# Window attention on one core: scores and query-key in 64x64 tiles, relative bias added by VectorE, maximum subtracted by GpSimd

## The chip, the cores and the metric

The kernel runs on 1 core of one Trainium2 chip. The time is device microseconds of one execution; the measure is the median over several executions of the same program. Everything is in 32-bit floats. In the text PE is TensorE, DVE is VectorE, ACT is ScalarE, POOL is GpSimd and SP is SyncE, which here only issues DMAs.

## What is computed

One transformer block with 8x8 windows on an image batch `x` of 4x48x128x128, and behind it an inverted-bottleneck convolution. The change touches only the attention of the first block (window size `ws` 8, 4 heads of 12 channels, 64 tokens a window):

```
h = _layernorm(xf, norm1_g, norm1_b)            # then cut into windows: (windows, 64, 48)
qkv = h @ qkv_w.T + qkv_b
q, k, v = (qkv[0] * scale, qkv[1], qkv[2])
attn = jnp.einsum('whnd,whmd->whnm', q, k)
attn = attn + rpb_table[rel_idx].transpose(2, 0, 1)[None]
attn = jax.nn.softmax(attn, axis=-1)
o = jnp.einsum('whnm,whmd->whnd', attn, v)
o = o.transpose(0, 2, 1, 3).reshape(B_, N, C) @ proj_w.T + proj_b
xf = shortcut + o                               # windows put back
m = _layernorm(xf, norm2_g, norm2_b)
xf = xf + gelu(m @ fc1_w.T + fc1_b) @ fc2_w.T + fc2_b
...
x + bn(conv1x1(relu(bn(dwconv3x3(relu(bn(conv1x1(x))))))))
```

## The kernel before

The program has three stages one after another: `attention`, `mlp`, and the convolution. `attention` works on 128 groups of 8 windows (512 tokens). A group is 4 pairs of windows; a pair fills the 128 partitions with its 2x64 tokens. Each engine has its own list of instructions, a function `step(i)` that is run for i = -4 to 130, with semaphores between the engines. In one step an engine works on several groups at different points of the pipeline: the layer norm of group i+4 and i+3, query and key of group i+2, the softmax of group i, the weighing of values of group i-1, the output of group i-2, and the second layer norm of group i-3. The order inside a step is written out by hand. The first ten steps (-4 to 5) and the last nine are written out; those between run in a loop of two steps (`schedule`, L200).

The steps that the change touches:

- *Query and key.* PE multiplies the normalized, transposed tokens `xnT` with `w_qk` (L369), two row tiles of 64 rows and 112 columns. The result is copied from PSUM twice: q by DVE into `qa` (L438), k by ACT into `kk` (L491).
- *Keys.* For the scores of all four heads in one matmul, the keys are laid out block by block: SP copies, with one DMA per head (L295), the 12 rows of a head from `kk` to the head's columns in `kb`, 12 partitions x 8 windows x 64 tokens.
- *Bias.* `kb` holds 128 rows: 64 of the bias, which are written once, and 48 of keys. `qa` holds an identity above q. So the matmul of the scores (L329), 128 rows by 64 columns, 256 moving columns, adds the bias itself. Eight such matmuls make the scores of a group in PSUM (`ps_s`, two banks), four at the end of the step before and four at the start of the group's own step.
- *Softmax.* DVE takes the maximum of each row of 64 from PSUM (L421) and subtracts it while it moves the scores into `prob` (L428). ACT takes the exponential in one instruction (L496). PE turns the probabilities (L317), ACT copies them out (L456), PE weighs the values (L381).
- *Others in a step.* ACT also copies the values (L465), the turned output `oT` (L469), the turned tokens `xnT` (L472), and makes the two steps of the layer norms (logarithm L475, root L484). PE turns the output (L339) and the tokens (L346), projects the output (L359), and makes the values (L388). POOL does four small products of the layer norms (L506, L511, L515, L520). SP stores the finished group (L290) and loads a coming one (L178).

A matmul in 32 bits is two instructions in the profile, a transpose is one.

Of the kernel before, what the change touches and what calls it, by code (L numbers as in the profile page):

```python
# [9 lines left out]
ALU = mybir.AluOpType  # L10
# [3 lines left out]
P = 128  # L14
# [5 lines left out]
ONE = 64  # L20
# [95 lines left out]
def attention(nc, d):  # L116

    with ExitStack() as ctx:
        sb = lambda n, s, t=F32: ctx.enter_context(nc.sbuf_tensor(n, s, t))
        sem = lambda n: ctx.enter_context(nc.semaphore(n))  # L120
        ident = sb("ident", [P, P])
        eps = sb("eps", [P, 1])
        w_qk, w_v, w_o = sb("w_qk", [P, 112]), sb("w_v", [P, 2 * C]), sb("w_o", [P, 2 * C])
        qkv_w, qkv_b = sb("qkv_w", [P, 3 * C]), sb("qkv_b", [1, 3 * C])
        lnrow, qk_row = sb("lnrow", [1, 3 * C]), sb("qk_row", [1, 112])
# [5 lines left out]
        cen, cen2 = ([sb(f"{n}{s}", [P, PAIRS, C]) for s in range(2)] for n in ("cen", "cenb"))  # L131
        sq = sb("sq", [P, 2 * PAIRS, C])
        xn = [sb(f"xn{s}", [P, PAIRS, ONE]) for s in range(2)]
        xnT = [sb(f"xnT{s}", [P, TOK // 2]) for s in range(2)]


        qa = [sb(f"qa{s}", [P, TOK]) for s in range(2)]
        kk = [sb(f"kk{s}", [P, TOK]) for s in range(2)]
        kb = [sb(f"kb{s}", [P, 2 * PAIRS, NH, NT]) for s in range(2)]
        vb = [sb(f"vb{s}", [P, PAIRS, 2, 2, 2 * VE]) for s in range(2)]  # L140
        top = [sb(f"top{s}", [P, PAIRS * NH]) for s in range(2)]
# [11 lines left out]
        ps_a, ps_b = psum[:, 6, :], psum[:, 7, :]  # L153
        ps_xT, ps_v, ps_y = ps_a[:, 0:TOK // 2], ps_a[:, 0:PAIRS * C], ps_a[:, TOK // 2:TOK // 2 + PAIRS * C]
        ps_o, ps_oT = ps_b[:, 0:PAIRS * NH * VE], ps_b[:, TOK // 2:TOK]

        w_loaded, fixed, w_bias, w_ready = sem("w_loaded"), sem("fixed"), sem("w_bias"), sem("w_ready")
        ident_put, lnrow_put, row_put, rows_loaded = sem("ident_put"), sem("lnrow_put"), sem("row_put"), sem("rows_loaded")
# [7 lines left out]
        xnT_ready, xnT_copied, qk_ready, q_copied, k_copied = (  # L166
            sem(n) for n in ("xnT_ready", "xnT_copied", "qk_ready", "q_copied", "k_copied"))
        v_ready, v_copied, s_ready, top_done, sub_done, exp_done = (
            sem(n) for n in ("v_ready", "v_copied", "s_ready", "top_done", "sub_done", "exp_done"))
# [6 lines left out]
        def load_x(eng, g, s):  # L176

            eng.dma_start(xtok[:, bass.ds(g, 1), :, :], d["x_tokens"][:, bass.ds(g, 1), :, :]).then_inc(x_loaded[s], 16)  # L178

        def x_loads(g, s):  # L180

            return 8 * (g - s) + 16

        def x_of(g):
            return xtok[:, bass.ds(g, 1), :, :].rearrange("q g p c -> q (g p) c")

        def keys_of(i, s):

            return 16 * NH // 2 * (i - s) + 16 * NH

        def halves(t):

            return t.rearrange("q (a e t) -> q e a t", e=2, t=P)

        W_FIXED, FIXED = 3, 23

        def has(g):
            return not isinstance(g, int) or 0 <= g < GROUPS

        def schedule(eng, step, begin=None, at=0):  # L200

            for i in range(-4, 6):
                if begin and i == at:
                    begin(eng)
                step(i, i % 2)
            with eng.Fori(6, GROUPS - 7, 2) as i:
                step(i, 0)
                step(i + 1, 1)
            for i in range(GROUPS - 6, GROUPS + 3):
                step(i, i % 2)  # L210
# [3 lines left out]
        def shift_rows(pe):  # L214

            pe.wait_ge(w_loaded, 16 * W_LOADS)
            nc.tensor.matmul(ps_a[0:1, 0:3 * C], ln_b[:, :], qkv_w[0:C, :], start=True, stop=True).then_inc(w_bias, 1)
# [4 lines left out]
        def put_bias(eng, write, half):  # L222

            eng.wait_ge(looked_up, 1)
            eng.wait_ge(fixed, FIXED)
            cols = slice(NT // 2 * half, NT // 2 * half + NT // 2)
            found = psum[NT * half:NT * half + NT, half, 0:NH * NT // 2].rearrange("q (h m) -> q h m", h=NH)
            for s in range(2):
                write(kb[s][0:NT, :, :, cols], bc(found, 1, 2 * PAIRS)).then_inc(bias_put, 1)
# [1105 lines left out]
```

## Time and profile before

| | |
|---|---|
| median of 3 executions | 1934.54 us (1932.46 to 1935.5) |
| the profiled execution, its own time | 1930.68 us |
| its span, first to last instruction | 1928.8 us |
| PE busy over the span | 1834.6 us (95%) |
| DVE busy | 1447.5 us (75%) |
| ACT busy | 1307.4 us (68%) |
| POOL busy | 646.9 us (34%) |
| DMA queue q1 (SP and ACT issues) | 282114 packets, 189.12 MB |

The attention takes about the first 770 us of the span, the MLP stage the stretch to about 1050, and the convolution the rest. The shares of busy time over the span are averages over these three stages; what the change does is read from the first one alone. An engine's busy time counts instructions; the time that SP spends on issuing DMAs isn't counted as busy and is read from the rows of the DMA issues.

### The profile page before, as it was taken

How to read it: one execution, taken by the hardware profiler on the slowest of the kernel's cores; microseconds unless marked ns; L12 is line 12 of the kernel's file. 1: busy time of each engine (PE TensorE's matmuls, PEld its weight loads, DVE VectorE, ACT ScalarE, POOL GpSimd, SP SyncE). 2: the span in 40 equal slices, each digit the busy share in tenths (PEclk: the TensorE clock that was granted, in tenths of full speed). 3: DMA queues.
4: the chain of work that ended last, by engine and by line, in shares of the span. 5: the costliest groups of instructions: out<-in, count | busy, mean ns of one | idle time of the engine just before them, and what ended most of it. 6: DMA issues, size and time to landing. Idle time of an engine off the chain costs nothing.

```text
span 1928.8 us, 75776 instructions
## 1 busy us (share of the span) xinstructions
PE 1834.6 (95%) x30980; PEld 1570.3 (81%) x30980; DVE 1447.5 (75%) x2649; ACT 1307.4 (68%) x2838; POOL 646.9 (34%) x869
## 2 busy tenths in 40 slices
PE   5999999999999998789998999999999999999998
PEld 4888888888888886456666899999999999999997
DVE  5999999999999998667777566566566566566564
ACT  2888888888888786445555666666666666666665
POOL 4333333333333332502201443334243352343240
PEclk9999999999999999799999999999999999999999
DMA  2222222222222221778875354445364454545331
GB/s 68 69 74 76 74 77 74 77 77 74 78 73 78 73 78 64 163 182 186 184 176 130 83 136 103 98 132 107 96 146 94 115 121 105 111 128 102 101 109 35
DMA packets 286378, 198.91 MB, mean 103 GB/s; under 512 B 225928, under 2 KB 275610, under 8 KB 276442
## 3 DMA queue, kind: packets, MB, share of 16 engines
q1 hardware_dynamic: 282114, 189.12, 38.8%
q0 software_dynamic: 2368, 6.25, 1.7%
q8 instruction: 174, 2.85, 0.6%
q10 hardware_dynamic: 1688, 0.42, 0.1%
q14 instruction: 34, 0.28, 0.0%
HBM read 128.39 MB, written 54.72 MB: 95 GB/s over the span
## 4 chain that ended last, share of the span: by engine, by line
PE 51%; DMA 4%; ACT 2%; DVE 1%; issue 1%; SPq 0%; ACTq 0%; DVEq 0%
PE psum L1112 14%; PE psum L1131 14%; PE psum L1157 10%; PE psum L1166 5%; PE psum L632 3%; DMA room<-tok_mid 3%; PE psum L647 2%; PE psum L659 2%; ACT h2T L1213 1%; ACT h L870 1%; DVE room L697 0%; DVE room L708 0%; SPq L607 0%; ACTq L720 0%; DVE room L871 0%
## 5 line engine op out<-in xcount | busy, mean ns | idle before, releaser
L920 POOL TENSOR_TENSOR mats<-mats,dscale 112x2048 f32<-112x2048 f32 x72 | 260.8, 3622 | 315.9 <-DMA mats<-in_taps 313.3
L1112 PE MATMUL psum<-ew,xp 64*100 64x96 f32 x6144 | 322.2, 252 | 15.9 <-ACT h L870 13.6
L871 DVE TENSOR_SCALAR h<-psum 100x384 f32<-100x384 f32 x384 | 212.0, 557 | 150.2 <-PE psum L1112 138.3
L1112 PEld LDWEIGHTS psum<-ew,xp 64*100 64x100 f32 x6144 | 295.4, 165 | 25.2 <-ACT h L870 18.7
L1213 ACT ACTIVATE h2T<-psum 96x1024 f32<-96x1024 f32 x192 | 195.6, 1019 | 176.2 <-PE psum L1166 176.2
L1131 PE MATMUL psum<-h,mats 101*64 101x128 f32 x4608 | 269.3, 274 | 1.6 <-issue 0.9
L1131 PEld LDWEIGHTS psum<-h,mats 101*64 101x64 f32 x4608 | 252.0, 137 | 11.9 <-issue 2.0
L870 ACT ACTIVATE room<-psum 64x512 f32<-64x512 f32 (+1 forms) x384 | 206.1, 537 | 78.0 <-PE psum L1131 71.6
L329 PE MATMUL psum<-kb,qa 128*64 128x256 f32 x2048 | 244.0, 380 | 0.8 <-DVE prob L428 0.8
L871 DVE TENSOR_SCALAR room<-psum 64x512 f32<-64x512 f32 (+1 forms) x288 | 174.3, 605 | 64.7 <-PE psum L1131 58.8
L870 ACT ACTIVATE h<-psum 100x384 f32<-100x384 f32 x384 | 186.6, 486 | 48.4 <-PE psum L1112 34.2
L1157 PE MATMUL psum<-h2T,pw 128*64 128x128 f32 x3072 | 194.4, 276 | 9.1 <-ACT h2T L1213 9.0
L329 PEld LDWEIGHTS psum<-kb,qa 128*64 128x64 f32 x2048 | 140.7, 138 | 56.3 <-issue 1.9
L1157 PEld LDWEIGHTS psum<-h2T,pw 128*64 128x64 f32 x3072 | 167.2, 137 | 20.3 <-ACT h2T L1213 13.4
L511 POOL TENSOR_TENSOR xn<-cen,rstd 128x192 f32<-128x192 f32 x128 | 64.9, 507 | 338.8 <-ACT rstd L484 338.8
L421 DVE TENSOR_REDUCE top<-psum 128x16 f32<-128x1024 f32 x128 | 156.8, 1225 | 6.9 <-PE psum L329 4.7
L428 DVE TENSOR_TENSOR prob<-psum,top 128x1024 f32<-128x1024 f32 x128 | 155.9, 1218 | 0.1
L894 POOL COPY xp<-piece 128x400 f32<-128x400 f32 x128 | 67.5, 528 | 256.5 <-DMA piece<-img_mid 241.1
L456 ACT ACTIVATE probT<-psum 128x512 f32<-128x512 f32 x256 | 151.2, 601 | 0.0
L381 PEld LDWEIGHTS psum<-vb,probT 128*64 128x64 f32 x4096 | 129.9, 138 | 18.6 <-issue 1.2
L381 PE MATMUL psum<-vb,probT 128*64 128x26 f32 x4096 | 143.4, 219 | 1.6 <-issue 1.0
L496 ACT ACTIVATE prob<-prob 128x1024 f32<-128x1024 f32 x128 | 135.3, 1057 | 4.6 <-DVE prob L428 1.6
(150 smaller groups left out, 3125.9 us busy)
## 6 DMA issues: line engine op xcount, KB each, us to landing
mats<-in_taps SPq DMA_DIRECT2D x69, 896.0 KB, 6.0
tok_mid<-mid SPq DMA_DIRECT2D x128, 224.0 KB, 1.9
room<-tok_mid SPq DMA_DIRECT2D x64, 448.0 KB, 5.1
piece<-img_mid SPq DMA_DIRECT2D x196, 63.8 KB, 2.3
img_mid<-room SPq DMA_DIRECT2D x128, 97.5 KB, 3.8
kb<-kk SPq DMA_DIRECT2D x512, 24.0 KB
out<-yc SPq DMA_DIRECT2D x32, 384.0 KB, 4.5
scratch<-in_x_tokens SPq DMA_DIRECT2D x126, 96.0 KB, 2.0
```

Source lines behind the costliest of these rows:

```text
L329: mm = nc.tensor.matmul(ps_s[NT * w:NT * w + NT, p // 2, 256 * (p % 2):256 * (p % 2) + 256], qa[s][:, NT * n:NT * n + NT], kb[s][:, n, :, ...
L381: mm = nc.tensor.matmul(ps_o[NT * w:NT * w + NT, at:at + 2 * VE], probT[:, p, h, NT * w:NT * w + NT], vb[1 - s][:, p, h, w, :], start=True ...
L421: nc.vector.tensor_reduce(top[s][:, :], sc, AX_X, ALU.max).then_inc(top_done, 1)
L428: nc.vector.tensor_tensor(prob[s][:, :, :], sc, bc(top[s][:, :], 2, NT), ALU.subtract)\
L456: nc.scalar.activation(probT[:, 2 * k:2 * k + 2, :, :].rearrange("q p h n -> q (p h n)"), ps_p[:, k, :], ACT.Copy)\
L870: return nc.scalar.activation(dst, src, ACT.Relu)
L871: return nc.vector.tensor_scalar(dst, src, 0.0, None, ALU.max)
L920: nc.gpsimd.tensor_tensor(m, m, bc(scale[0:MROWS, at:at + TCH], 2, POUT), ALU.mult).then_inc(mats_scaled, 1)
L1112: mm = nc.tensor.matmul(ring[(j + u) % 4][0:PIN, p:4 * CH:4], xp[hx][rows, 2 * j + p, :], w1[rows, c, :], start=True, stop=True)
L1131: mm = nc.tensor.matmul(bank[:, n % 4:4 * PATCHES:4], mats[ch // TCH][0:PIN + 1, ch % TCH, :], h1[0:PIN + 1, ch, :], start=True, stop=True)
L1157: mm = nc.tensor.matmul(ps_y[n % 2][64 * r:64 * r + 64, at:at + PCOLS], w2[:, c, :], h2T[n % 2][:, r, at:at + PCOLS], start=True, stop=True)
L1213: nc.scalar.activation(h2T[n % 2][0:CH, :, :], turned_at(n, last)[0:CH, :, 0:POUT * PART], ACT.Copy).then_inc(copied, 1)
```

## The change

In `attention` alone:

- `qa`, `kk` and the identity rows go. Query-key (`queries_keys`) is four matmuls of 64 rows by 64 columns with 256 moving columns. They leave, in `kq`, for the even pairs and the odd pairs on opposite halves of the partitions, q on one half and k on the other. ACT copies all of it in one instruction.
- `kb` keeps only keys, with one half of the partitions per parity of the pair. SP lays them out with eight DMAs a group instead of four, 12 rows of 256 contiguous elements each.
- The scores (`scores`) are eight matmuls of 64 rows by 64 columns, 256 moving columns. They are all made in one place, a whole step ahead.
- The bias is looked up as before into a tile `bias`; DVE adds it while it moves the scores from PSUM into `prob`, takes the maximum from there, and POOL subtracts it in place. ACT takes the exponential in one instruction a group, as before.
- The order in a step is another on PE, ACT, DVE and POOL; query and key, and the first layer norm, run one step further ahead (i+3, i+4, i+5), with three buffers for `cen` and `xnT`. All steps, -5 to 130, are written out: the loop goes.

```diff
+        kq = [sb(f"kq{s}", [P, 2, TOK // 2]) for s in range(2)]
+        kb = [sb(f"kb{s}", [P, NH, PAIRS, NT]) for s in range(2)]
+        bias = sb("bias", [P, NH, NT])
...
-            for i in range(-4, 6):
...
-            with eng.Fori(6, GROUPS - 7, 2) as i:
-                step(i, 0)
-                step(i + 1, 1)
...
+            for i in range(-5, GROUPS + 3):
+                if begin and i == -1:
                     begin(eng)
+                step(i)
...
         @block.sync
...
-                if has(i + 2):
-                    sp.wait_ge(k_copied, i + 3)
+                if has(i + 3):
+                    s = (i + 3) % 2
+                    sp.wait_ge(kq_copied, i + 4)
                     for h in range(NH):
-                        r = slice(ONE + HD * h, ONE + HD * h + HD)
-                        sp.dma_start(kb[s][r, :, h, :], kk[s][r, :].rearrange("q (n m) -> q n m", m=NT))\
-                            .then_inc(keys_put[s], 16)
+                        for e in range(2):
+                            k_at, b_at = ONE * (1 - e) + HD * h, ONE * e + HD * h
+                            sp.dma_start(kb[s][b_at:b_at + HD, h, :, :].rearrange("q n m -> q (n m)"),
+                                         kq[s][k_at:k_at + HD, e, :]).then_inc(keys_put[s], 16)
...
         @block.tensor
...
-                        mm = nc.tensor.matmul(ps_s[NT * w:NT * w + NT, p // 2, 256 * (p % 2):256 * (p % 2) + 256],
-                                              qa[s][:, NT * n:NT * n + NT], kb[s][:, n, :, :], start=True, stop=True)
...
+            def scores(g):
+                pe.wait_ge(keys_put[g % 2], of_parity(g, KEYS))
+                wait(pe, add_done, g)
+                for a in range(QUAD):
+                    for e in range(2):
+                        r = slice(ONE * e, ONE * e + ONE)
+                        for w in range(2):
+                            at = P * a + NT * w
+                            mm = nc.tensor.matmul(ps_s[NT * w:NT * w + NT, e, 256 * a:256 * a + 256],
+                                                  kq[g % 2][r, e, at:at + NT], kb[g % 2][r, :, 2 * a + w, :], start=True, stop=True)
+                mm.then_inc(s_ready, 1)
+            def queries_keys(g):
+                pe.wait_ge(xnT_copied, g + 1)
+                for half in range(2):
+                    for e in range(2):
+                        r = slice(ONE * e, ONE * e + ONE)
+                        part = ONE if half != e else 0
+                        mm = nc.tensor.matmul(ps_k[ONE * half:ONE * half + ONE, e, :], w_qk[r, part:part + ONE], xnT[g % 3][r, :],
                                               start=True, stop=True)
+                mm.then_inc(qk_ready, 1)
...
         @block.vector
...
+                if has(i):
+                    dve.wait_ge(s_ready, i + 1)
+                    nc.vector.tensor_tensor(prob[i % 2][:, :, :].rearrange("q (p h) m -> q p (h m)", h=NH),
+                                            ps_s.rearrange("q e (a n) -> q (e a) n", a=QUAD),
+                                            bc(bias[:, :, :].rearrange("q h m -> q (h m)"), 1, PAIRS), ALU.add).then_inc(add_done, 1)
...
+                    nc.vector.tensor_reduce(top[i % 2][:, :], prob[i % 2][:, :, :], AX_X, ALU.max).then_inc(top_done, 1)
...
-                    nc.vector.tensor_reduce(top[s][:, :], sc, AX_X, ALU.max).then_inc(top_done, 1)
...
-                    nc.vector.tensor_tensor(prob[s][:, :, :], sc, bc(top[s][:, :], 2, NT), ALU.subtract)\
-                        .then_inc(sub_done, 1)
...
-                    nc.vector.tensor_copy(halves(qa[s][ONE:ONE + C, :]), ps_k[0:C, :, :].rearrange("q e (a t) -> q e a t", t=P))\
-                        .then_inc(q_copied, 1)
...
         @block.scalar
...
-                    nc.scalar.activation(halves(kk[s][ONE:ONE + C, :]),
-                                         ps_k[ONE:ONE + C, :, :].rearrange("q e (a t) -> q e a t", t=P), ACT.Copy)\
-                        .then_inc(k_copied, 1)
...
+                    act.wait_ge(qk_ready, g + 1)
+                    nc.scalar.activation(kq[g % 2][:, :, :], ps_k, ACT.Copy).then_inc(kq_copied, 1)
...
         @block.gpsimd
...
+                    pool.wait_ge(top_done, i + 1)
+                    blocks = prob[i % 2][:, :, :]
+                    nc.gpsimd.tensor_tensor(blocks, blocks, bc(top[i % 2][:, :], 2, NT), ALU.subtract).then_inc(sub_done, 1)
```

SP's queue over two steps of the attention before, in the loop (`kk`, `kb` keys, `scratch` the tokens, `tok_mid` the stored group):

```order
L290 DMA tok_mid<-mid 128x448
L292 REGISTER_ALU
L295 DMA kb<-kk 12x8x64 x4
L298 REGISTER_ALU
L178 ISA
L178 DMA scratch<-in_x_tokens 128x192
L289 REGISTER_ALU
L290 ISA
L290 DMA tok_mid<-mid 128x448
L292 REGISTER_ALU
L295 DMA kb<-kk 12x8x64 x4
```

and over two steps of the change:

```order
L275 DMA tok_mid<-mid 128x448
L282 DMA kb<-kq 12x256 x8
L181 DMA scratch<-in_x_tokens 128x192
L275 DMA tok_mid<-mid 128x448
L282 DMA kb<-kq 12x256 x8
```

Ten DMAs stand in a step where there were six, the keys between the store and the load as before.

PE over one step before, from the end of one group's scores on (`prob` probabilities, `on` output, `xn` tokens of the layer norm, `vb` values):

```order
L339 MATMUL psum<-ident,on 128x128 x2
L342 REGISTER_ALU
L346 MATMUL psum<-ident,xn 128x128 x2
L55 ISA
L317 MATMUL psum<-ident,prob 128x128 x8
L359 MATMUL psum<-w_o,oT 128x96 x2
L369 MATMUL psum<-xnT,w_qk 112x128 x4
L381 MATMUL psum<-vb,probT 64x26 x16
L388 MATMUL psum<-w_v,xnT 64x96 x4
L325 ISA
L329 MATMUL psum<-kb,qa 64x256 x4
```

and over one step of the change:

```order
L305 MATMUL psum<-ident,prob 128x128 x4
L312 MATMUL psum<-ident,on 128x128 x2
L305 MATMUL psum<-ident,prob 128x128 x4
L321 MATMUL psum<-w_o,oT 128x96 x2
L330 MATMUL psum<-ident,xn 128x128 x2
L342 MATMUL psum<-kb,kq 64x256 x8
L353 MATMUL psum<-xnT,w_qk 64x256 x4
L366 MATMUL psum<-vb,probT 64x26 x16
L378 MATMUL psum<-w_v,xnT 64x96 x4
```

The turned probabilities, which wait for the exponential, moved to the head of the step, and the scores moved from the step's ends to between the turned tokens and query-key.

ACT over one step before (`kk` keys, `lnv` and `rstd` of the layer norms):

```order
L465 ACTIVATE vb<-psum 64x8x12 x4
L469 ACTIVATE oT<-psum 128x256
L472 ACTIVATE xnT<-psum 128x256
L475 ACTIVATE lnv<-sqs,eps 128x8
L456 ACTIVATE probT<-psum 128x512
L484 ACTIVATE rstd<-lnv 128x8
L456 ACTIVATE probT<-psum 128x512
L491 ACTIVATE kk<-psum 48x2x2x128
L496 ACTIVATE prob<-prob 128x1024
```

and over one step of the change (`kq` queries and keys):

```order
L477 ACTIVATE vb<-psum 64x8x12 x4
L481 ACTIVATE oT<-psum 128x256
L463 ACTIVATE probT<-psum 128x512 x2
L489 ACTIVATE lnv<-sqs,eps 128x8
L493 ACTIVATE xnT<-psum 128x256
L497 ACTIVATE kq<-psum 128x512
L504 ACTIVATE rstd<-lnv 128x8
L469 ACTIVATE prob<-prob 128x1024
```

The copies of the turned probabilities moved ahead of the layer norm, the root moved behind the copy of queries and keys, and the exponential stays last.

## Rows read from the trace of the kernel before

**Rows 1.** Stretches: length, busy us (count) of PE, PEld, DVE, ACT, POOL; clock; DMA, GB/s.
```profile
400.00:500.00 100.00, 100.00 (x1402) 81.41 (x1400) 97.57 (x195) 80.52 (x216) 34.14 (x71) 1.00 0.24 75
...
760.00:800.00 40.00, 20.60 (x228) 14.29 (x228) 21.97 (x48) 12.27 (x29) 28.46 (x59) 0.70 0.51 130
```

**Rows 2.** Order of time, DVE's maximum: start, us, engine, line, operation, tiles [idle before].
```profile
51.40 1.23 DVE L421 TENSOR_REDUCE top<-psum 128x16 f32<-128x1024 f32 x1 [0.90 <-PE psum L329]
...
751.58 1.22 DVE L421 TENSOR_REDUCE top<-psum 128x16 f32<-128x1024 f32 x1 [0.21 <-PE psum L329]
```

**Rows 3.** Order of time over one step of the attention, several engines.
```profile
398.96 1.06 ACT L496 ACTIVATE prob<-prob 128x1024 f32<-128x1024 f32 x1
...
399.30 3.30 SPq L295 DMA_DIRECT2D kb<-kk  x4
...
400.04 1.03 ACT L465 ACTIVATE vb<-psum 64x96 f32<-64x96 f32 x4
...
401.54 0.25 PEld L346 LDWEIGHTS psum<-ident,xn 128*128 128x128 f32 x2
...
401.85 0.38 ACT L469 ACTIVATE oT<-psum 128x256 f32<-128x256 f32 x1 [0.77 <-PE psum L339]
...
401.86 1.04 PE L317 MATMUL psum<-ident,prob 128*128 128x128 f32 x8
...
402.12 0.38 ACT L472 ACTIVATE xnT<-psum 128x256 f32<-128x256 f32 x1
...
402.63 0.53 PEld L359 LDWEIGHTS psum<-w_o,oT 128*128 128x128 f32 x4
...
403.06 0.22 ACT L484 ACTIVATE rstd<-lnv 128x8 f32<-128x8 f32 x1
...
403.25 0.49 PEld L369 LDWEIGHTS psum<-xnT,w_qk 64*112 64x112 f32 x8
...
404.07 0.59 ACT L491 ACTIVATE kk<-psum 48x512 f32<-48x512 f32 x1 [0.31 <-PE psum L369]
...
405.19 1.90 PE L329 MATMUL psum<-kb,qa 128*64 128x256 f32 x16
```

**Rows 4.** Order of time at the end of the attention, ACT and PE.
```profile
765.59 0.38 ACT L469 ACTIVATE oT<-psum 128x256 f32<-128x256 f32 x1 [2.40 <-PE psum L339]
...
766.03 0.52 PEld L359 LDWEIGHTS psum<-w_o,oT 128*128 128x128 f32 x4 [0.71 <-ACT oT L469]
```

**Rows 5.** DMA issues by line: ns min/median/max of one issue, first and last start.
```profile
L295 SPq DMA_DIRECT2D kb<-kk x512: 778/785/968, 32.5 to 751.6; - x171
...
L290 SPq DMA_DIRECT2D tok_mid<-mid x128: 332/349/360, 59.9 to 770.2; - x128
...
L178 SPq DMA_DIRECT2D scratch<-in_x_tokens x126: 346/364/517, 18.7 to 730.4; - x126
...
L607 SPq DMA_DIRECT2D img_mid<-room x128: 302/403/1242, 795.8 to 1052.7; - x128
...
L259 ACTq DMA_DIRECT2D w_qk<-qk_row x2: 619/623/627, 18.5 to 19.8; - x2
...
L726 ACTq DMA_DIRECT2D room<-room x2: 565/589/613, 783.4 to 784.0; - x2
```

**Rows 6.** Order of time in the MLP stage, PE.
```profile
902.58 1.53 PE L632 MATMUL psum<-room 64*64 64x256 f32 x24
```

**Rows 7.** Groups of instructions, 150 to 650 us and whole run: busy us, mean ns | idle.
```profile
L428 DVE TENSOR_TENSOR prob<-psum,top 128x1024 f32<-128x1024 f32 x89 | 108.4, 1218 | 0.0
...
L438 DVE COPY qa<-psum 48x512 f32<-48x512 f32 x89 | 60.9, 684 | 2.8
...
L506 POOL TENSOR_TENSOR sq<-cenb 128x192 f32<-128x192 f32 x89 | 45.0, 506 | 103.7 <-DVE cenb L444 103.7
...
L920 POOL TENSOR_TENSOR mats<-mats,dscale 112x2048 f32<-112x2048 f32 x72 | 260.8, 3622 | 315.9 <-DMA mats<-in_taps 313.3
```

**Rows 8.** Order of time before the first group, PE, the look-ups of the bias.
```profile
15.73 13.82 PE L109 MATMUL psum<-table,scratch 128*64 128x4 f32 x256 [4.86 <-DVE scratch L98]
```

More of the change, by code:

```diff
@@ L319, in turn_probs @@
                 mm.then_inc(pT_ready, 1)
-            def scores(i, s, part):
-                if has(i):
-                    if part == 0:
-                        pe.wait_ge(q_copied, i + 1)
-                        pe.wait_ge(keys_put[s], keys_of(i, s))
-                        wait(pe, sub_done, i)
-                    for n in range(PAIRS * part, PAIRS * part + PAIRS):
-                        p, w = divmod(n, 2)
-                        mm = nc.tensor.matmul(ps_s[NT * w:NT * w + NT, p // 2, 256 * (p % 2):256 * (p % 2) + 256],
-                                              qa[s][:, NT * n:NT * n + NT], kb[s][:, n, :, :], start=True, stop=True)
-                    if part:
-                        mm.then_inc(s_ready, 1)
@@ new lines, in turn_out, with project @@
+            def turn_out(g):
+                pe.wait_ge(on_done, g + 1)
+                for a in range(QUAD):
+                    mm = nc.tensor.transpose(ps_oT[:, P * a:P * a + P], on[:, 2 * a:2 * a + 2, :], ident[:, :])
+                mm.then_inc(oT_ready, 1)
+            def project(g):
+                pe.wait_ge(oT_copied, g + 1)
+                if has(g + 2):
+                    pe.wait_ge(v_copied, g + 3)
+                for a in range(QUAD):
+                    mm = nc.tensor.matmul(ps_y[:, 2 * C * a:2 * C * a + 2 * C], oT[:, P * a:P * a + P], w_o[:, :],
+                                          start=True, stop=True)
+                mm.then_inc(y_ready, 1)
@@ L392, in step, with values @@
-                scores(i + 1, 1 - s, 0)
-            schedule(pe, step, lambda pe: pe.wait_ge(bias_put, 4), -1)
+                                mm = nc.tensor.matmul(ps_o[NT * w:NT * w + NT, at:at + 2 * VE],
+                                                      probT[:, QUAD * e + a, h, NT * w:NT * w + NT],
+                                                      vb[g % 2][:, p, h, w, :], start=True, stop=True)
+                mm.then_inc(o_ready, 1)
+            def values(g):
+                wait(pe, res_done, g - 2)
+                wait(pe, v_copied, g)
+                for a in range(QUAD):
+                    for w in range(2):
+                        at = P * a + NT * w
+                        mm = nc.tensor.matmul(ps_v[NT * w:NT * w + NT, 2 * C * a:2 * C * a + 2 * C], xnT[g % 3][:, at:at + NT],
+                                              w_v[:, :], start=True, stop=True)
+                mm.then_inc(v_ready, 1)
@@ new lines, in step @@
+            def step(i):
+                if has(i - 1):
+                    turn_probs(i - 1, 0)
+                if has(i - 2):
+                    turn_out(i - 2)
+                if has(i - 1):
+                    turn_probs(i - 1, 1)
+                if has(i - 2):
+                    project(i - 2)
+                if has(i + 3):
+                    turn_tokens(i + 3)
+                if has(i + 1):
+                    scores(i + 1)
+                if has(i + 3):
+                    queries_keys(i + 3)
+                if has(i - 1):
+                    weigh(i - 1)
+                if has(i + 1):
+                    values(i + 1)
```

298 lines of the change are left out of this document (124 added, 174 removed).

## Prediction, made before the change was run

> **What bounds the kernel now.** I read the stretches first, then the spacing of one instruction over the attention, then one step in order of time, then the DMA issues. In the attention the stretches show two engines full at once: in 100 us PE is busy for 100.00, DVE for 97.57, ACT for 80.52 and POOL for 34.14, at a granted clock of 1.00, the upper level, 2.4 GHz [rows 1]. The row-maximum reduction runs once per group: for group 2 it starts at 51.40, for group 126 at 751.58, so a step takes 700.18 / 124 = 5.65 us [rows 2]. In the step itself the exponential has slack: it ends at 400.02, and PE turns those probabilities only at 401.86 [rows 3]. The SP queue has slack too: four key transfers take 3.30 us, the store 0.35 and the load 0.36, together 4.0 of 5.65 [rows 3, 5]. The change takes work from PE and DVE, and it adds work in just the two places that had slack.
>
> **The change, part by part, for one step.**
>
> *PE.* The scores before are 16 instructions in 1.90 us, two column tiles side by side [rows 3]. Now they stand on 64 rows and 64 columns. The program already has that form in its MLP stage: 24 instructions of 64x64 with 256 columns take 1.53 us from first start to last end, where two at a time they would need 24/16 of 1.90, or 2.85 [rows 3, 6]. So four do run side by side. Scores (16) and query-key (8) together make exactly these 24, hence 1.53. Before, scores took 1.90 and query-key's weight loads alone 0.49 [rows 3]. PE loses 1.90 + 0.49 - 1.53, about 0.9 us a step, and stops being full.
>
> *DVE.* The subtraction (1.22) and the copy of q (0.68) go [rows 7]. The bias addition reads the same 128x1024 from PSUM and is taken at the subtraction's 1.22. The maximum now reads SBUF and is kept at 1.23 [rows 2]. Net 0.68 less, so DVE falls from 5.5 (97.57% of 5.65) to 4.8 a step.
>
> *POOL.* It gains the subtraction of 128x1024. Its rows are 192 columns in 0.51 and 2048 columns in 3.62 [rows 7]; on the line between them 1024 columns take 1.90. With its four others POOL comes to 3.9 of 5.65: no bound. The subtraction lies between the maximum and the exponential. By the ring counted below, the scores of a group end 3.4 after one exponential and the group's own exponential starts 4.8 after the next, 7.2 later; addition, maximum and subtraction take 4.35 of that, so the rest of DVE's queue fits between them.
>
> *ACT.* The copy of k (48x512, 0.59) becomes a copy of q and k (128x512), taken at the same 0.59 [rows 3]. The exponential is the same piece as before.
>
> *A ring of one step.* PE now opens a step with the turned probabilities, which wait for the exponential, and it does scores and query-key before it weighs the values; ACT copies kq, and only then comes the next exponential. From the end of one exponential to the end of the next: 0.02 to the start of the value copies, these 1.03, the copy of oT 0.38 [rows 3], hand-over to PE 0.06 (765.97 to 766.03) [rows 4], output projection 0.62 (402.63 to 403.25), the two token transposes 0.25 [rows 3], the 24 instructions 1.53 [rows 6], hand-over 0.06, copy of kq 0.59, root 0.22, exponential 1.06 [rows 3]. Sum 5.82. Two ACT instructions can overlap by 0.11 (402.12 against an end of 402.23) [rows 3]; with three such places and 0.09 of the projection that overlaps its neighbour, the shortest ring is 5.4. So even without anything else a step costs 5.4 to 5.8, about what it costs now. What PE and DVE gain is swallowed there.
>
> *SP's queue.* Four key transfers a group become eight, each 12 rows of 1 KB instead of 12 rows of 8 pieces. No row shows this shape, so its issue is bounded. From below: 0.30 to 0.40, for 48 rows of 8 pieces from SBUF to DRAM, or 0.35 for the plain store. From above: the key transfer itself, 0.785, with the same rows, engine and both ends in SBUF [rows 5]. Between them lie the transfers within SBUF whose row is one contiguous run, issued on ACT's queue: 0.623 and 0.589 [rows 5]. I take their mean, 0.606, since they share with the new one both the two ends in SBUF and the contiguous row; the key row keeps the extra pieces. Between two issues lie 0.05 (3.30 less 4 x 0.785, over 3) [rows 3, 5]. A step then needs 8 x 0.656 = 5.25, the store 0.40, and the load 0.57 (0.517, its longest, issued right behind another) [rows 5]: 6.22 us. That is longer than the ring, and nothing hides it, since scores wait for the keys and the keys are issued two steps ahead at most. The queue becomes the bound if one issue exceeds (5.65 - 0.97) / 8 - 0.05 = 0.535.
>
> *Loop and ends.* The loop is written out. The steps around the loop were written out already; nothing is charged for the rest. The bias copies of 64x1024 shrink and some memsets go, while the first keys come later; PE's look-ups hold the first group until 29.5 either way [rows 8]. Taken as 0, within 3 us.
>
> *Sum.* 124 steps x (6.22 - 5.65) = +71 us, on the profiled execution's 1930.7: 2002. That execution lies 0.2% under the median of the three times, 1934.5, which is also about what a measurement can tell from no change (4 us).
>
> **A rule against this.** The rows say that the number of pieces doesn't set an issue: 384 pieces take 0.30 to 0.40, 96 take 0.785 [rows 5]. The Trainium skill, "Perfetto Trace Analysis", section "What 'DMA-bound' means", says that where an issuing sequencer is solid DMA, large descriptors are what matters. By that rule eight transfers of 12 large pieces would be cheap, and the time would be that of the second or third rival below. The trace so far speaks against it as the whole account.
>
> **The rivals.**
> 1. *The issue keeps its full price.* If what makes the key transfer dear is its 12 rows, an issue stays at 0.785: 8 x 0.835 + 0.97 = 7.65, and 124 x 2.00 = +248: 2179. For it: the same 12 rows, and it is the dearest steady issue on SP. Against: the one-run rows at 0.6.
> 2. *The ring decides, at its summed length.* With an issue under 0.535 SP drops out, and 5.82 gives 124 x 0.17 = +21: 1952. For it: most SP issues are 0.30 to 0.43. Against: none of them goes from SBUF to SBUF.
> 3. *Faster.* The issue is cheap and the ring runs at its shortest, 5.4: 124 x -0.25 = -31: 1900. One mechanism, the overlap of neighbouring instructions on ACT and PE in the ring; it decides from a step below 5.62. For it: such overlaps are in the rows. Against: the waits between engines stand there too.
>
> That the 64x64 tiles don't run four at a time is excluded by rows 6. A fall of PE's clock is not priced: the mean fell to 0.70, part of the time at 1.2 GHz, where PE was busy for 20.6 of 40 us [rows 1], and PE keeps 4.8 (5.65 less 0.9) of 6.2.
>
> **How the numbers follow.** The queue as the bound with an issue of 0.54 to 0.70: 0.35, the likeliest, 2002. Rival 1: 0.22. Rival 2: 0.12 slower. A step within 0.03 of today's: 0.07. Rival 3: 0.24. Slower is 0.35 + 0.22 + 0.12 = 0.69, same 0.07, faster 0.24. The range goes from 1912, which leaves out the shorter half of rival 3, to 2180, the upper bound of the issue. The likeliest case alone spans 1935 to 2095.
>
> **What would show it.** Right: SP's queue nearly solid over the attention, each key issue near 0.6, scores starting when their keys land, PE busy for about three quarters, a step near 6.2. Rival 1 shows the same with 0.785 and a step of 7.6. Rivals 2 and 3 show an SP queue with gaps, PE waiting at the turned probabilities for the exponential, and ACT waiting for query-key. I am wrong as well if the wait in front of the exponential is POOL's subtraction (then it costs well over 1.9), or if DVE is still full.

## The result and the profile after

The change takes 2156.29 us (2151.65 to 2159.21, 4 executions) against 1934.55 of the kernel before (1932.46 to 1935.5, 4 executions): 1.1145 times the time, 95% interval 1.113 to 1.1161. The profiled execution takes 2157.2 us, its span is 2155.4. Forecast were 2002, with 1912 to 2180 as the range: the right sign and the right mechanism, at under a third of the size (+67 against +222).

DVE's maximum in the changed kernel, in order of time, for groups 2 and 126; these answer to [rows 2]:

```profile
57.63 1.21 DVE L422 TENSOR_REDUCE top<-prob 128x16 f32<-128x1024 f32 x1
...
970.97 1.21 DVE L422 TENSOR_REDUCE top<-prob 128x16 f32<-128x1024 f32 x1
```

A step takes (970.97 - 57.63) / 124 = 7.37 us; it was 5.65. That is 124 x 1.72 = 213 us. Group 2 comes 6.2 us later (51.40 before). SP's first key issues, in the changed kernel and in the one before:

```profile
32.68 6.15 SPq L282 DMA_DIRECT2D kb<-kq  x8
```

```profile
32.50 3.46 SPq L295 DMA_DIRECT2D kb<-kk  x4
```

They start at the same time and last 2.7 us longer, and the next two groups are slow steps like all others. Together that is 219 of the span's 226.6. So the loss lies in the steps of the attention.

The stretch that answers to [rows 1], with the same columns:

```profile
400.00:500.00 100.00, 77.90 (x1112) 56.46 (x1105) 64.53 (x139) 59.90 (x163) 52.18 (x69) 0.93 0.20 60
```

No engine is full any more: PE fell from 100 to 78, DVE from 98 to 65, ACT from 81 to 60. The granted clock is 0.93, no longer steadily at the upper level, in an engine that is idle for a fifth of the time. What is full is the queue that counts in no busy share. Order of time in the changed kernel, SP:

```profile
398.92 0.43 SPq L275 DMA_DIRECT2D tok_mid<-mid  x1
399.39 6.05 SPq L282 DMA_DIRECT2D kb<-kq  x8
405.49 0.51 SPq L181 DMA_DIRECT2D scratch<-in_x_tokens  x1
406.05 0.43 SPq L275 DMA_DIRECT2D tok_mid<-mid  x1
406.52 6.75 SPq L282 DMA_DIRECT2D kb<-kq  x8
```

Each row starts 0.04 to 0.06 after the one before ends: SP doesn't wait. From the first key issue to the last, only ten gaps between its issues are longer than 0.1, the longest 0.42. A step is 6.05 + 0.51 + 0.43 and the gaps, 7.13, and 7.8 where one of the eight issues is a long one, as in the last row. The DMA issues by line (ns, smallest, median, largest of one issue) answer to [rows 5]:

```profile
L282 SPq DMA_DIRECT2D kb<-kq x1024: 713/714/2176, 32.7 to 971.3; - x171
...
L181 SPq DMA_DIRECT2D scratch<-in_x_tokens x126: 323/509/1227, 17.8 to 944.1; - x126
...
L275 SPq DMA_DIRECT2D tok_mid<-mid x128: 319/429/1612, 72.6 to 993.9; - x128
```

The key issue takes 0.714, not the forecast 0.606. Its mean is 0.745, since 38 of the 1024 take over 1 us. The other engines of the changed kernel, in order of time; they answer to [rows 3]:

```profile
401.18 0.36 DVE L435 TENSOR_TENSOR mid<-psum,scratch 128x192 f32<-128x192 f32 x1 [3.02 <-DMA tok_mid<-mid]
...
401.40 0.60 ACT L497 ACTIVATE kq<-psum 128x512 f32<-128x512 f32 x1 [1.59 <-PE psum L353]
...
402.51 1.22 DVE L409 TENSOR_TENSOR prob<-psum,bias 128x1024 f32<-128x1024 f32 x1
...
405.48 1.90 POOL L521 TENSOR_TENSOR prob<-prob,top 128x1024 f32<-128x1024 f32 x1 [1.14 <-DVE top L422]
...
406.65 1.09 PE L342 MATMUL psum<-kb,kq 64*64 64x256 f32 x16 [0.51 <-DMA kb<-kq]
```

The durations are those that were taken: addition 1.22, subtraction 1.90, copy 0.60. The scores start behind the keys, 16 of them in 1.09 us when all the keys are there. But the longest waits are not those of the scores. Groups of instructions, whole run (busy us, mean ns | idle):

```profile
L435 DVE TENSOR_TENSOR mid<-psum,scratch 128x192 f32<-128x192 f32 x128 | 45.8, 358 | 320.7 <-DMA tok_mid<-mid 309.6
L342 PE MATMUL psum<-kb,kq 64*64 64x256 f32 x2048 | 166.7, 449 | 67.5 <-DMA kb<-kq 67.0
```

DVE waits 309.6 us for stores: each stands in SP's queue behind eight keys, and DVE may not overwrite `mid` before it has landed. So one full queue shows up as waits for several different tiles, whatever passes through it.

### The profile page after: what moved, and what is told of

It reads as the page before. It is cut to its first block, busy times and chain, and to the rows that moved or that the text cites. A ratio compares the mean times of both kernels' runs of the same rounds, so it can differ in the third digit from the quotient of the medians.

```text
span 2155.4 us, 72654 instructions
## 1 busy us (share of the span) xinstructions
PE 1857.2 (86%) x30980; PEld 1515.5 (70%) x30980; DVE 1340.8 (62%) x2520; ACT 1287.5 (60%) x2840; POOL 884.1 (41%) x995
## 4 chain that ended last, share of the span: by engine, by line
PE 45%; DMA 4%; ACT 2%; DVE 1%; issue 1%; SPq 0%; ACTq 0%; DVEq 0%
PE psum L1128 13%; PE psum L1147 12%; PE psum L1173 9%; PE psum L1182 5%; DMA room<-tok_mid 4%; PE psum L648 3%; PE psum L675 2%; PE psum L663 2%; ACT h2T L1229 1%; ACT h L886 0%; DVE room L724 0%; SPq L623 0%; DVE room L713 0%; DMA room<-in_ident 0%; DVE room L887 0%
## 5 line engine op out<-in xcount | busy, mean ns | idle before, releaser
L521 POOL TENSOR_TENSOR prob<-prob,top 128x1024 f32<-128x1024 f32 x128 | 243.5, 1903 | 139.4 <-DVE top L422 139.4
L435 DVE TENSOR_TENSOR mid<-psum,scratch 128x192 f32<-128x192 f32 x128 | 45.8, 358 | 320.7 <-DMA tok_mid<-mid 309.6
L342 PE MATMUL psum<-kb,kq 64*64 64x256 f32 x2048 | 166.7, 449 | 67.5 <-DMA kb<-kq 67.0
L497 ACT ACTIVATE kq<-psum 128x512 f32<-128x512 f32 x128 | 76.5, 598 | 242.2 <-PE psum L353 242.2
L305 PE MATMUL psum<-ident,prob 128*128 128x128 f32 x1024 | 171.7, 294 | 36.3 <-ACT prob L469 35.8
L526 POOL TENSOR_TENSOR sq<-cen 128x192 f32<-128x192 f32 x128 | 70.6, 552 | 293.9 <-DVE cen L447 293.9
L366 PEld LDWEIGHTS psum<-vb,probT 128*64 128x64 f32 x4096 | 135.4, 143 | 56.7 <-issue 56.0
L305 PEld LDWEIGHTS psum<-ident,prob 128*128 128x128 f32 x1024 | 122.0, 148 | 59.1 <-ACT prob L469 56.5
L342 PEld LDWEIGHTS psum<-kb,kq 64*64 64x64 f32 x2048 | 74.8, 152 | 122.8 <-DMA kb<-kq 92.8
```

Of the source, the lines that this page charges most:

```text
L305: mm = nc.tensor.transpose(ps_p[:, e, at:at + P], prob[g % 2][:, blocks:blocks + 2, :], ident[:, :])
L342: mm = nc.tensor.matmul(ps_s[NT * w:NT * w + NT, e, 256 * a:256 * a + 256], kq[g % 2][r, e, at:at + NT], kb[g % 2][r, :, 2 * a + w, :], st ...
L366: mm = nc.tensor.matmul(ps_o[NT * w:NT * w + NT, at:at + 2 * VE], probT[:, QUAD * e + a, h, NT * w:NT * w + NT], vb[g % 2][:, p, h, w, :], ...
L521: nc.gpsimd.tensor_tensor(blocks, blocks, bc(top[i % 2][:, :], 2, NT), ALU.subtract).then_inc(sub_done, 1)
```

## The experiments

The kernel before ran beside each batch and had its own median there: 1930.05 (the first four kernels), 1936.12 (the next three), 1935.76, 1938.06 and 1938.51. A "step" below is always measured at DVE's maximum as above. half_keys and half_keys_root leave out half of the key transfers, and dram12 reads other rows in place of the keys: their times show what bounds, and are no versions to use. The key issues counted are those on SP. Taken together:

| kernel | time, us | ratio to before [95%] | step | key issue, median | over 1 us |
|---|---|---|---|---|---|
| before | 1930 to 1939 | | 5.65 | 0.785 | 0 of 512 |
| the change | 2156.29 | 1.1145 [1.113, 1.1161] | 7.37 | 0.714 | 38 of 1024 |
| half_keys | 1905.98 (one run) | 0.9875 | 5.46 | 0.720 | 12 of 512 |
| rows16 | 2046.01 | 1.0604 [1.0587, 1.0622] | 6.55 | 0.589 | 73 of 1024 |
| rows16_early | 2046.69 | 1.0606 [1.0589, 1.0624] | 6.56 | 0.589 | 71 of 1024 |
| before_split | 2234.04 (one run) | 1.1575 | 8.04 | 0.779 | 1 of 1024 |
| dram12 | 1914.66 (one run) | 0.9889 | 5.46 | 0.363 | 35 of 1024 |
| before_flat | 1936.58 | 1.0 [0.9988, 1.0011] | 5.65 | 0.786 | 16 of 512 |
| sp_loop | 2202.9 | 1.1393 [1.1371, 1.1415] | 7.72 | 0.714 | 42 of 1024 |
| mix62 | 1924.58 | 0.9939 [0.9923, 0.9956] | 5.54 | 0.589 | 54 of 768 |
| mix62_early | 1994.87 | 1.0302 [1.0282, 1.0323] | 6.11 | 0.589 | 36 of 768 |
| mix62_later | 1935.93 | 0.9989 [0.9976, 1.0001] | 5.66 | 0.589 | 50 of 768 |
| mix62_root | 1932.84 | 0.9971 [0.9959, 0.9982] | 5.61 | 0.589 | 50 of 768 |
| half_keys_root | 1898.3 | 0.9793 [0.9774, 0.9811] | 5.33 | 0.720 | 17 of 512 |

**half_keys: is it the queue?** The change with every second key transfer left out.

```diff
-        KEYS = 16 * 2 * NH
+        KEYS = 16 * NH
...
-                        for e in range(2):
+                        for e in range(1):
```

> The change with only four of the eight key transfers of a group issued; the keys of the odd pairs stay zero, so their scores are the bias alone. If SP's queue is the bound: SP needs 4 x 0.76 + 0.97 = 4.0 us a step, drops out, and the step becomes that of the ring from exponential to exponential, 5.4 to 5.8 us: 1900 to 1955 us. If the time came from something else (POOL's subtraction, DVE's addition, the written-out loop, the clock): near 2156.

Measured: 1905.98, a step of 5.46. With four issues fewer the change is faster than the kernel before by 24 us, in one run. So the whole loss is the queue's, and the rest of the change is a gain once the queue is out of the way. The price of an issue is not made by a full queue that pushes back: here the queue has room, and its issues by line are as dear as in the change:

```profile
L282 SPq DMA_DIRECT2D kb<-kq x512: 713/720/1518, 32.7 to 726.8; - x171
```

One step of half_keys in order of time shows what bounds then:

```profile
400.24 0.60 ACT L497 ACTIVATE kq<-psum 128x512 f32<-128x512 f32 x1 [1.04 <-PE psum L353]
400.74 0.20 ACT L504 ACTIVATE rstd<-lnv 128x8 f32<-128x8 f32 x1
400.84 1.05 ACT L469 ACTIVATE prob<-prob 128x1024 f32<-128x1024 f32 x1
...
401.94 0.66 PE L305 MATMUL psum<-ident,prob 128*128 128x128 f32 x4 [0.35 <-ACT prob L469]
...
403.28 0.69 PE L321 MATMUL psum<-w_o,oT 128*128 128x96 f32 x4
...
404.12 1.09 PE L342 MATMUL psum<-kb,kq 64*64 64x256 f32 x16
...
405.03 0.61 PE L353 MATMUL psum<-xnT,w_qk 64*64 64x256 f32 x8
```

PE waits for the exponential, ACT's copy waits for query-key, and the exponential waits behind the copy and the root. That is the ring of the prediction, of which 5.46 lies near the shortest length (5.4).

**rows16: is it the twelve rows?** Each head's keys stand on 16 rows, four of them empty, so that a transfer has 16 rows of 1 KB.

```diff
...
-                            k_at, b_at = ONE * (1 - e) + HD * h, ONE * e + HD * h
+                            k_at, b_at = ONE * (1 - e) + HP * h, ONE * e + HP * h
...
```

> The change with each head padded to 16 rows in w_qk, kq and kb (zero columns in w_qk), so a key transfer has 16 rows of 1 KB instead of 12; still eight a group. If the 12 rows make the issue dear: an issue falls from 0.714 to the 0.35 to 0.50 of the other transfers, SP needs 8 x 0.45 + 0.97 = 4.6 us, and the ring decides: 1900 to 1955 us. If the two ends in SBUF make it dear: an issue stays at 0.6 to 0.7, and the time stays at 2060 to 2156.

Measured: 2046.01, between the two expectations and nearer to the second. The issues of its keys by line:

```profile
L290 SPq DMA_DIRECT2D kb<-kq x1024: 507/589/2325, 32.6 to 867.3; - x171
```

Four rows more make the issue 0.125 shorter (0.507 for one with a gap ahead of it). Rows are a part of the price, not most of it. The Trainium skill, "DMA: Bandwidth & Descriptors", section "Why a DMA increments its semaphore by 16 and not by 1", says that a transfer runs on the largest number of engines, up to 16, that divides both sides' outer size, and that the issuing sequencer itself writes the increments that are missing to 16. By that rule 12 rows run on 12 engines and leave four increments to SP; 16 rows leave none. The 0.125 agrees in sign, but dram12 below has 12 rows at half the price, so no run here shows that those writes are what costs.

**before_split: is it the number of issues alone?** The kernel before with each key transfer cut in two halves of 12 rows by 4 pieces.

```diff
+                        for c in range(2):
+                            n = slice(PAIRS * c, PAIRS * c + PAIRS)
-                        sp.dma_start(kb[s][r, :, h, :], ...
+                            sp.dma_start(kb[s][r, n, h, :], ...
```

> The kernel before with each of its four key transfers cut in two (12 rows of 4 pieces instead of 8), nothing else. If the queue of eight key issues alone makes the loss: an issue costs 0.71 to 0.79, SP needs 8 x 0.80 + 0.80 = 7.2 us a step against 5.65, and the time rises by 124 x 1.55 = 190 to about 2125 us. If the loss comes from the other parts of the change: 1935.

Measured: 2234.04, above the expected 2125 and worse than the change itself, a step of 8.04. Its issues by line, and one step of SP:

```profile
L297 SPq DMA_DIRECT2D kb<-kk x1024: 778/779/1074, 32.9 to 1058.7; - x171
```

```profile
400.54 0.35 SPq L290 DMA_DIRECT2D tok_mid<-mid  x1
401.00 6.60 SPq L297 DMA_DIRECT2D kb<-kk  x8
407.89 0.36 SPq L178 DMA_DIRECT2D scratch<-in_x_tokens  x1
408.52 0.34 SPq L290 DMA_DIRECT2D tok_mid<-mid  x1
```

Half the pieces, the same issue: 0.779 against 0.785, and where the issue stands behind another key issue the median is 0.779 in both kernels. A transfer of half the size costs SP as much. The change moves the same 12 KB per transfer as one piece a row instead of four and takes 0.714, so larger pieces save at most 0.065. From store to store 7.98 pass, of which the rows fill 7.31; the rest are gaps between them, in which SP does the loop's register work; the expectation had not counted them.

**rows16_early: does ACT's order matter while the queue binds?** rows16 with the exponential ahead of the copy of keys and queries.

```diff
+                if has(i):
+                    exps(i)
                 if has(i + 3):
                     g = i + 3
                     act.wait_ge(qk_ready, g + 1)
```

> As rows16, and on ACT the exponential of the step stands ahead of the copy of queries and keys instead of last. If the ring (exponential, turned probabilities, projection, scores, query-key, copy, exponential) decides once the queue is free: the copy and PE's wait for it leave the ring, and the step falls to what DVE or PE need, 4.9 to 5.3 us: 1840 to 1890 us. If the ring doesn't decide: the same time as rows16.

Measured: 2046.69, within 1 us of rows16. While the queue decides, it doesn't matter.

**dram12: is it the two ends on the core?**

```diff
+            keys_from = d["x_tokens"].rearrange("q g p c -> q (g p c)")[:, 0:TOK // 2]
...
-                                         kq[s][k_at:k_at + HD, e, :]).then_inc(keys_put[s], 16)
+                                         keys_from[k_at:k_at + HD, :]).then_inc(keys_put[s], 16)
```

> The change with the eight key transfers reading rows of the tokens in device memory (12 rows of 1 KB, as before) in place of the copy of the keys on the core, so the keys are not the reference's; all else, the waits too, is the change. If it is the two ends on the core that took the issue from the 0.606 of the forecast's one-run rows to 0.714, the issue falls to about 0.61, the step to 8 x 0.65 + 0.51 + 0.43 + 0.15 = 6.3 us plus the long issues' 0.25, and the time to about 2040 us. If the place of the source is nothing and only the rows count, the issue stays at 0.71, the step at 7.4 and the time at 2150 to 2160.

Measured: 1914.66, below both expectations. Its issues by line, and one step of SP:

```profile
L284 SPq DMA_DIRECT2D kb<-in_x_tokens x1024: 297/363/1927, 33.0 to 727.8; - x171
```

```profile
402.29 3.23 SPq L284 DMA_DIRECT2D kb<-in_x_tokens  x8
405.57 0.35 SPq L181 DMA_DIRECT2D scratch<-in_x_tokens  x1
```

The same 12 rows of 1 KB, read from device memory, are issued in 0.363, half of 0.714. Eight take 3.23 us, less than the four transfers of [rows 3], and the step is 5.46 again, that of half_keys. So the place of the source makes about half of the price, more than the theory said, and more than the 0.125 of the four rows.

**before_flat and sp_loop: where do the long issues come from?** The kernel before written out, and the change with SP alone in a loop:

```diff
-            for i in range(-4, 6):
...
-            with eng.Fori(6, GROUPS - 7, 2) as i:
...
+            for i in range(-4, GROUPS + 3):
```

> The kernel before with its loop of 57 passes written out, nothing else. Theory: the long key issues of over 1 us come with written-out code on SP, so some 30 to 50 of the 512 show here too, and SP's four issues of a step leave room for them: 1915 to 1935 us, no part of the change's loss. Rival: they come with eight issues and a full queue, so none shows here. Second rival: written-out code costs every engine, and the kernel is slower by over 1% (1950 or more).

```diff
-            schedule(sp, step)
...
+            with sp.Fori(7, GROUPS - 8, 2) as i:
+                step(i, 1)
+                step(i + 1, 0)
```

> The change with SP's steps 7 to 120 in a loop of two steps a pass, every other engine written out as in the change. Theory: the long issues come with SP's own written-out code, and nearly all go; the issue stays at 0.714 and the mean step comes from 7.39 to the old median of 7.13 plus some 0.2 for the loop's register work: 2130 to 2155 us. Rival: they are the queue's own pushing back, 30 to 40 of them stay, and the register work comes on top: 2170 to 2185.

Measured: before_flat 1936.58, no difference, with 16 long issues (fewer than expected); sp_loop 2202.9, above both of its expectations, with 42 long ones, so they are not from SP's own code. But the rival, the queue pushing back, isn't it either. A long issue of the changed kernel, and the DMA queues in 1.5 us around it (408.0 to 409.5; queue: packets, MB, share):

```profile
408.07 1.42 SPq L282 DMA_DIRECT2D kb<-kq  x1
```

```profile
q1 hardware_dynamic: 37, 0.02, 5.5%
q8 instruction: 1, 0.02, 3.9%
```

The 1.5 us before have no such packet. I take an instruction packet for 16 KB of code that some engine loads as it goes on. Beside every one of the 38 long issues (and of rows16's 73, before_flat's 16 and sp_loop's 42) one starts within 0.75 us of the issue's start. And whenever the long issue began, it ends shortly after its packet has ended: 0.18 to 0.41 us, median 0.39, over the 38. From 50 to 770 us the kernel before, before_flat and the change have:

```profile
q8 instruction: 8, 0.13, 0.1%
```

```profile
q8 instruction: 82, 1.34, 0.8%
```

```profile
q8 instruction: 62, 1.02, 0.6%
```

So the long issues come with written-out code. The steady distance of the ends suggests that such an issue waits for the code packet; no run takes the packets away and leaves the rest, so it isn't shown. A long one costs about 0.66 (mean 1.376), on average 8 x (0.745 - 0.714) = 0.25 a step where the queue is full; before_flat, whose queue has room, loses nothing. SP's loop costs more than it could save: the step goes from 7.37 to 7.72.

**mix62: a version to beat both.** Heads of 16 rows, six transfers on SP, two on POOL's queue.

```diff
...
+                if has(i + 3):
+                    pool.wait_ge(kq_copied, i + 4)
+                    for at in range(2 * NH - ON_POOL, 2 * NH):
+                        put_keys(pool, (i + 3) % 2, *divmod(at, 2), keys_put2)
```

> The change with heads of 16 rows and the last two of the eight key transfers of a step issued from POOL's queue, at the end of POOL's step, with a semaphore of their own that the scores wait for as well. SP: 6 x 0.63 + 0.58 + 0.43 + 0.15 + 0.3 for long issues = 5.3 us, below the ring's 5.47 of half_keys; POOL: 3.85 + 2 x 0.55 = 4.95. Theory (the queue was the only thing that held the change): the ring decides, step 5.5, about 1905 to 1920 us, faster than both kernels by 1%. Rival: POOL's two issues stand in the ring (the subtraction comes late behind them) or last far longer than 0.55, the step is 5.8 or more, and the time 1950 or more.

Measured: 1924.58, a step of 5.54. It is 0.6% faster than the kernel before, a small gain but clear of its interval, where 1% (1905 to 1920) was expected. Its issues by line:

```profile
L206 SPq DMA_DIRECT2D kb<-kq x768: 507/589/1910, 32.9 to 733.2; - x192
L206 POOL DMA_DIRECT2D kb<-kq x256: 501/522/662, 33.5 to 733.1; - x128
```

The Trainium skill, "Perfetto Trace Analysis", section "DMA Optimizations", advises to balance DMAs over the engines that can issue them where the issuing is the bottleneck. The traces agree: at 0.52 an issue on POOL, the 1.0604 of rows16, all on SP, becomes 0.9939.

**mix62_early: a shorter ring?** mix62 with the exponential first, as in rows16_early.

```diff
...
+                if has(i):
+                    exps(i)
                 if has(i + 3):
                     g = i + 3
                     act.wait_ge(qk_ready, g + 1)
...
-                if has(i):
-                    exps(i)
```

> mix62 with ACT's exponential ahead of its wait for the scores and query-key products, so that the copy of keys and queries and the root no longer stand in the ring ahead of it. Theory: with the queue out of the way the ring decides, and it gets shorter by the copy's 0.6 and the root's 0.2 at most, until SP's 5.3 or POOL's 5.0 decides: step 5.3, 1880 to 1900 us. Rival: the ring runs over other waits as long (PE 4.9 to 5.1 busy, POOL), and nothing is gained over mix62 (within 5 us).

Measured: 1994.87, 3.0% slower than the kernel before. Neither expectation holds. Order of time in mix62_early, POOL and ACT:

```profile
398.71 1.90 POOL L535 TENSOR_TENSOR prob<-prob,top 128x1024 f32<-128x1024 f32 x1
...
400.65 1.06 ACT L483 ACTIVATE prob<-prob 128x1024 f32<-128x1024 f32 x1 [0.64 <-POOL prob L535]
...
402.09 0.20 ACT L520 ACTIVATE rstd<-lnv 128x8 f32<-128x8 f32 x1
...
402.37 0.51 POOL L544 TENSOR_TENSOR mid<-cenb,rstd 128x192 f32<-128x192 f32 x1 [0.89 <-ACT rstd L520]
...
403.28 1.03 POOL L206 DMA_DIRECT2D kb<-kq  x2
...
404.79 1.90 POOL L535 TENSOR_TENSOR prob<-prob,top 128x1024 f32<-128x1024 f32 x1
```

A new ring: subtraction, exponential, copy, root, POOL's products that need the root, its two issues, next subtraction: 404.79 - 398.71 = 6.08. The root had come behind an exponential that waits for POOL.

**mix62_root and mix62_later: open that ring.** ACT takes root, exponential, copy; POOL's issues go one step later, ahead of its wait for the root. mix62_later has POOL's part alone, which is:

```diff
...
+                if has(i + 2):
+                    pool.wait_ge(kq_copied, i + 3)
+                    for at in range(2 * NH - ON_POOL, 2 * NH):
+                        put_keys(pool, (i + 2) % 2, *divmod(at, 2), keys_put2)
                 if has(i - 3):
                     s = (i - 3) % 2
                     pool.wait_ge(rstd_done, i + 5)
```

> mix62 with two moves. ACT takes the root, then the exponential, then the copy of keys and queries (mix62: copy, root, exponential; mix62_early: exponential, copy, root), and POOL issues its two key transfers one step later, between its two squares' multiply and its wait for the root, so that they stand in nobody's way. Theory: mix62_early lost because the root came behind the exponential, and so POOL, which waits for the root before it can come to its next subtraction, stood in one ring with ACT (subtraction 1.90, exponential 1.06, copy 0.58, root 0.20, POOL's three multiplies 1.54 and two issues 1.03: 6.3 at most, 6.08 seen). With the root first that ring is open, and the exponential no longer waits for the scores' and keys' products either; what is left is POOL's own 5.0, PE's 5.1 and SP's 5.3: 1870 to 1900 us. Rival: the wait of the exponential for the subtraction, with the copy behind it, is as long a ring by itself: 1920 or more.

> mix62 with POOL's two issues moved alone (one step later, ahead of its wait for the root), ACT's order as in the change. If the ring over the copy and the root decides (step 5.47 in three kernels that free the queue in three ways), nothing changes: 1915 to 1930 us. If POOL's issues stand in the way, the step shortens: under 1910.

Measured: 1932.84 and 1935.93, both worse than mix62 against the kernel before of their batch (0.9971 and 0.9989 against 0.9939). The theory of mix62_root fell: the move of POOL's issues makes the step 0.12 longer (5.54 to 5.66), and ACT's order takes only 0.05 of that back (5.61). Waits from 150 to 650 us, of mix62 and of mix62_later (us in total, times, longest):

```profile
DVE mid L449 <- DMA tok_mid<-mid: 14.3, 26, 1.0
```

```profile
DVE mid L449 <- DMA tok_mid<-mid: 70.1, 87, 2.2
```

POOL's product for the store now comes behind its two issues, so the store comes later in SP's queue, and DVE waits for it. That this wait makes the whole 0.12 isn't shown.

**half_keys_root: the same order of ACT without POOL's issues.** half_keys (half of the key transfers left out), with the copy of keys and queries moved behind root and exponential on ACT.

```diff
...
-                if has(i + 3):
-                    g = i + 3
-                    act.wait_ge(qk_ready, g + 1)
-                    nc.scalar.activation(kq[g % 2][:, :, :], ps_k, ACT.Copy).then_inc(kq_copied, 1)
                 if has(i + 4) or has(i - 3):
                     act.wait_ge(ln_done, i + 5)
...
                 if has(i):
                     exps(i)
+                if has(i + 3):
+                    g = i + 3
+                    act.wait_ge(qk_ready, g + 1)
+                    nc.scalar.activation(kq[g % 2][:, :, :], ps_k, ACT.Copy).then_inc(kq_copied, 1)
```

> half_keys (every second key transfer left out, so half of the pairs see no keys) with ACT's order root, exponential, copy of keys and queries in place of copy, root, exponential. Theory (the ring exponential, turned probabilities, projection, scores, query-key, copy of keys and queries, root, exponential is what holds the step at 5.47 once the queue is free): the exponential no longer waits for the query-key products, the ring opens, and PE's own 93% of 5.47 = 5.1 us or DVE's 4.8 decides: step 5.1 to 5.3, 1860 to 1885 us. Rival: another ring as long holds it (POOL's subtraction comes 0.68 us late behind the maximum): step 5.4 or more, 1900 or more.

Measured: 1898.3, a step of 5.33, against 5.46 of half_keys: the ring opens, though the step and the time are above the expected 5.3 and 1885. The stretch 400 to 500 us (columns as in [rows 1]):

```profile
400.00:500.00 100.00, 95.37 (x1509) 71.92 (x1501) 92.64 (x187) 83.62 (x224) 71.89 (x96) 1.00 0.23 74
```

PE and DVE are near full again, at a clock of 1.00. They need 0.954 x 5.33 = 5.1 and 0.926 x 5.33 = 4.9 a step.

## Why the prediction was right and wrong

- *What would bound:* right. The queue is nearly solid, scores follow their keys, PE is busy for 78% ("about three quarters"), and half_keys, dram12 and mix62, which free the queue in three ways, are all faster than the kernel before: nothing else made the change slower.
- *The step that failed: "I take their mean, 0.606".* The two rows were transfers of a single row, issued on ACT; the new one has 12 rows, on SP. It measured 0.714, with gaps of 0.043: 8 x (0.757 - 0.656) = +0.81 a step. The reasons given, both ends on the core and a contiguous row, were right as far as they go (a source in device memory halves the price, dram12; one piece instead of four takes off at most 0.065), but the rows were left out (four more take off 0.125, rows16). How the missing 0.108 splits between the rows and the issuing engine stays open, since no run issues the new transfer on ACT. The upper bound, 0.785, turned out to be nearer.
- *Not priced at all: the long issues,* +0.25 a step. "The loop is written out ... nothing is charged for the rest" failed here. The kernel before could not show it: it has 8 code packets between its first and last key issue, where the change has 80, and no long issue. Load and store add 0.06 to their two terms (0.553 and 0.473 with their gaps, against 0.57 and 0.40: the store, now right behind the load, takes 0.43 instead of 0.35). Sum 6.22 + 0.81 + 0.25 + 0.06 = 7.34; measured 7.37.
- *Rival 1* came nearer in time (2179), by luck: its reason, the 12 rows, is the smaller part, and the same 12 rows cost 0.363 from device memory.
- *Rivals 2 and 3, the ring:* it exists (half_keys_root opens it), and it runs near its shortest, at 5.46. Faster by 1% is what the change gives where the issue is cheap: 1914.66 in dram12, one run, between 1900 and 1952. The threshold of 0.535 fits too: dram12 lies below it, rows16 above it.
- *Terms that held:* subtraction 1.90 (taken 1.90), addition 1.22 (1.22), maximum 1.21 (1.23), copy 0.60 (0.59), four tiles at a time (scores 1.09 and query-key 0.61, which overlap: 1.52 from 404.12 on in half_keys, taken 1.53). PE's whole step was taken at 4.8 and is 5.1 in half_keys_root, which decides nothing while the queue is full.
- *Loop and ends:* "0, within 3 us" was 6.2 at group 2. It is the queue once more, which is full from its first key issue on.
- *The rule weighed:* eight transfers of large pieces were not cheap. Half the pieces change nothing (before_split) and pieces four times as large save at most 0.065 of 0.779; the trace was right to speak against it as the whole account.

## What to carry to other kernels

Before cutting transfers into more, price one issue on the queue that is to take them: its number times its price is a bound like an engine's, though no busy share shows it. Take the price from a row that shares the ends, the rows and the neighbours, and where there is none, keep the nearest dearer row as the likeliest until a run shows otherwise: here 0.785 would have missed by 0.07, and 0.606 missed by 0.11. When an instruction is moved ahead in one engine's order, list what then stands behind it: with the root behind the exponential, mix62_early is 3.7% slower than mix62.

## What the runs showed that was not expected

- A transfer of 12 rows of 1 KB is issued on SP in 0.714 us with both ends on the core and in 0.363 with the source in device memory; 16 rows on the core take 0.589, and 0.507 with a gap ahead.
- The plain load is issued in 0.35 right behind issues from device memory (dram12) and in 0.51 right behind issues on the core (the change). With a gap of 0.2 to 0.5 ahead of it, it is 0.35 behind issues on the core too (sp_loop). Cause open.
- Half as many pieces change the median of an issue by 0.006 (before_split).
- An issue that is long beside an instruction packet takes 1.376 on average in place of 0.714. Which engine's packet it was stays open, and so does why some packets have no long issue beside them: between the first and the last key issue 80 such packets start in the change and 80 in rows16, with 38 and 73 long key issues.
- Which of the three in rows16 against the change costs the 0.125, the row count, the divisor or the increments, wasn't tried apart.
